# Value products of an attention step: two visits instead of three in a hand-written TensorE order

## The reference

```
x = x + attention(layernorm(x))      # 16 heads of 8 channels, causal, ALiBi
x = x + ffn(layernorm(x))            # gate, 8 experts, all of them summed
attention: scores = q k^T / sqrt(8) + slope_h * key position, causal mask, softmax, times v, w_proj
ffn: logits = z gate_w^T + b, rms-normed, softmax at temperature 0.5, the top gate g;
     y = sum over experts of (gelu(z w1_e + b1_e) w2_e + b2_e) * g / (g + 1e-6)
```

## Time and profile before

| what | value |
|---|---|
| time, median of 3 runs | 320.37 us (320.12 to 320.97) |
| profiled execution, its time | 320.51 us |
| its span, first to last instruction | 318.7 us |
| busy: PE, DVE, ACT, POOL | 296.8, 205.4, 193.7, 85.5 us |
| mean granted TensorE clock | 0.963 of full speed |
| value products L795 on PE | 512 matmul records, 42.3 us busy |
| chain that ended last: PE, DVE | 78%, 11% of the span |

### The profile page before, as it was taken

One profiled execution on the slowest core, in us unless ns is written; L12 is line 12 of the kernel. 1 busy time (PEld: TensorE's weight loads), 2 busy tenths in 40 slices (PEclk: granted clock), 3 DMA queues, 4 the chain that ended last, 5 costly groups with the idle time before them and its releaser, 6 DMA issues.

```text
span 318.7 us, 5649 instructions
## 1 busy us (share of the span) xinstructions
PE 296.8 (93%) x1830; PEld 195.8 (61%) x1831; DVE 205.4 (64%) x817; ACT 193.7 (61%) x323; POOL 85.5 (27%) x213
## 2 busy tenths in 40 slices
PE   7658799999969999999999999999999999999993
PEld 2535456666646666667666676657666765657871
DVE  5538489777877768554877786556776721267871
ACT  6561244646447568758567396857487877535462
POOL 3449321511133055002321172020300500700250
PEclk9795599999999999999999999999999999999998
DMA  6254300130300013002200131002001000000101
GB/s 185 90 148 143 117 2 0 44 114 5 101 18 0 2 38 126 1 0 54 66 5 0 34 97 66 2 17 69 0 4 36 1 4 0 2 0 1 33 2 33
DMA packets 12525, 13.24 MB, mean 42 GB/s; under 512 B 2064, under 2 KB 9104, under 8 KB 12240
## 3 DMA queue, kind: packets, MB, share of 16 engines
q1 hardware_dynamic: 11376, 11.70, 11.9%
q0 software_dynamic: 1024, 1.05, 1.6%
q10 hardware_dynamic: 96, 0.13, 0.2%
HBM read 5.14 MB, written 1.05 MB: 19 GB/s over the span
## 4 chain that ended last, share of the span: by engine, by line
PE 78%; DVE 11%; DMA 3%; issue 2%; POOL 2%; ACT 1%; SPq 1%; DVEq 0%; POOLq 0%; ACTq 0%
PE ffn_bank L863 14%; PE a_ring L770 12%; PE v_ring L748 12%; PE pv_bank L795 11%; PE a_ring L776 5%; PE a_ring L696 5%; DVE unused L1101 5%; PE a_ring L698 4%; PE a_ring L697 4%; DMA q_stack<-q_lo 1%; PE v_ring L824 1%; DMA q_stack<-m_lo 1%; PE v_ring L757 1%; PE v_ring L808 1%; DMA x_in<-x 1%
## 5 line engine op out<-in xcount | busy, mean ns | idle before, releaser
L1101 DVE CUSTOM_DVE_ANT_0 unused<-v_ring,cst 128x512 bf16<-128x512 f32 (+3 forms) x256 | 112.1, 487 | 51.8 <-PE v_ring L748 47.5
L570 ACT ACTIVATE probs<-a_ring 128x512 f32<-128x512 f32 (+1 forms) x192 | 92.3, 526 | 67.1 <-PE a_ring L776 66.0
L748 PE MATMUL v_ring<-k_stack,q_stack 128*128 128x512 f32 (+3 forms) x256 | 88.3, 416 | 5.4 <-DMA q_stack<-q_lo 3.2
L770 PE MATMUL a_ring<-q_stack,k_stack 128*128 128x512 f32 (+3 forms) x256 | 76.2, 357 | 2.0 <-DMA q_stack<-m_lo 2.0
L748 PEld LDWEIGHTS v_ring<-k_stack,q_stack 128*128 128x128 f32 x256 | 48.4, 205 | 25.9 <-issue 15.8
L587 ACT ACTIVATE hidden<-a_ring,cols_sb 128x512 f32<-128x512 f32 x64 | 43.3, 688 | 29.4 <-PE a_ring L698 29.0
L863 PE MATMUL ffn_bank<-hidden,w_sb 128*128 128x512 f32 x100 | 51.9, 604 | 0.9 <-ACT hidden L587 0.9
L770 PEld LDWEIGHTS a_ring<-q_stack,k_stack 128*128 128x128 f32 x256 | 46.0, 194 | 9.5 <-issue 5.6
L776 PE MATMUL a_ring<-score_mask,ident_bf 128*128 128x128 bf16 (+1 forms) x192 | 47.8, 250 | 0.0
L795 PE MATMUL pv_bank<-probs,v_ones 128*32 128x256 f32 (+3 forms) x512 | 42.3, 440 | 0.0
L334 POOL DMA_DIRECT2D k_stack<-k_lo x32 | 18.1, 568 | 56.4 <-PE a_ring L776 51.7
(11 more groups left out here) (123 smaller groups left out, 346.9 us busy)
## 6 DMA issues: line engine op xcount, KB each, us to landing
q_stack<-q_hi SPq DMA_DIRECT2D x8, 256.0 KB
k_stack<-k_hi SPq DMA_DIRECT2D x60, 32.0 KB
x_in<-x SPq DMA_DIRECT2D x4, 256.0 KB, 3.4
hidden<-w SPq DMA_DIRECT2D x1, 1024.0 KB, 7.8
k_stack<-k_lo POOLq DMA_DIRECT2D x32, 32.0 KB, 2.2
q_stack<-q_lo SPq DMA_DIRECT2D x4, 256.0 KB
w_sb<-w SPq DMA_DIRECT2D x1, 1024.0 KB, 5.1
x_res<-x SPq DMA_DIRECT2D x4, 256.0 KB, 2.9
```

What stands on the lines that cost most here:

```text
L570: act.activation(probs[:, n % 2, q, KIND_AT[kind]:KIND_AT[kind] + cols], a_bank()[:, 0:cols], ACT.Exp).then_inc(e_freed, 1)
L748: last = pe.matmul(dst[:, at:at + P * (n + 1)], q_stack[b % 2][:, s, n * P:(n + 1) * P], k_stack[:, s, q, 0:P * (n + 1)], start=True, stop ...
L770: pe.matmul(dst[:, at:at + P * (TB - j)], k_stack[:, s, q, j * P:(j + 1) * P], q_stack[b % 2][:, s, j * P:T], start=(at == 0), stop=False, ...
L1101: ins = dve.tensor_tensor_reduce(unused[:, (uses[0] - 1) % V_BANKS, at:at + cols], bank_[:, at:at + cols], cst[:, C_MASK + T - cols:C_MASK ...
```

## The change

Kinds 1 and 2 of a set's value products are both emitted at place 0 of the next step, one after the other, so that a set has two visits to the value product: kind 0 in its own step, kinds 1 and 2 in the next. Kind 0, which EARLY_PLAN had at place 11, is at place 12 in both plans.

```diff
 EARLY_PLAN = {
     "max": (-1, 0, 2, 3, 4, 5, 6, 8, 8, 9, 11, 11), "take_max": (12,),
-    "exp": (4, 4, 5, 6, 8, 8, 9, 11, 11, 13, 14, 14), "pv": (11, 15), "pv_last": (0,),
+    "exp": (4, 4, 5, 6, 8, 8, 9, 11, 11, 13, 14, 14), "pv": (12,), "pv_last": (0, 0),
 }
 LATER_PLAN = {
     "max": (-1, -1, 2, 3, 4, 5, 6, 7, 8, 9, 10, 11), "take_max": (13,),
-    "exp": (4, 5, 6, 7, 8, 9, 10, 10, 12, 13, 14, 15), "pv": (12, 15), "pv_last": (0,),
+    "exp": (4, 5, 6, 7, 8, 9, 10, 10, 12, 13, 14, 15), "pv": (12,), "pv_last": (0, 0),
 }
...
                         for kind in planned(b, s, k, "pv"):
                             pv(b, s, kind)
-                        if planned(b, s, k, "pv_last") and n >= 1:
-                            pv((n - 1) // SETS, (n - 1) % SETS, KINDS - 1)
-            pv(B - 1, SETS - 1, KINDS - 1)
+                        for i in planned(b, s, k, "pv_last"):
+                            if n >= 1:
+                                pv((n - 1) // SETS, (n - 1) % SETS, 1 + i)
+            pv(B - 1, SETS - 1, 1)
+            pv(B - 1, SETS - 1, 2)
```

## The result

The changed kernel took 321.81 us in the median of 20 runs, the kernel before beside it 320.74 us; the ratio is 1.0036 with an interval of 1.0024 to 1.0048, which is 0.8 to 1.5 us more. The forecast was 322.5 us, +2.0 by its sum. The profiled execution took 322.29 us with a span of 320.5 us, which is 1.8 us longer than the span before; but of these 0.77 lie ahead of all that was changed: the mask matmul of exponential unit 8 in step 0 starts at 42.43 instead of 41.66, and up to there both lists of PE are the same. From that start to the end of the span are 278.07 us, before 318.7 - 41.66 = 277.04: the change itself costs **1.03 us** in the trace; spans are printed to 0.1 us, so this is good to about 0.05.

What follows compares the result with a forecast made beforehand. PE was taken to bound the kernel from 95.8 us, PE and DVE in turn in steps 0 to 4. Terms 0.40 + 1.17 + 0.42 + 0.55 + 0 - 0.52 = +2.02 gave 322.5 us, range 321.0 to 323.7.

Steps and rivals of the forecast that it cites:

- the case of no change: Whole kernel: a difference under 0.3% (0.96 us), not to be told from none; chance 0.13.
- signs of being wrong: Prediction wrong if the transpose of maxima doesn't wait or step 1 loses under 1 us; too low if PE's clock falls.
- the rival in which DVE's backlog holds the start of step 2: DVE's backlog in step 1, not q, leads: the 1.17 goes, +0.85, 321.4 us; within the no-change chance of 0.13.
- step 0: Kind 0 behind the transpose +0.82 on PE, merged boundary -0.26, DVE's hole of 0.09 taken up: about +0.40 us.
- step 1: Kind 0's whole visit falls uncovered behind the transpose, making q's projection late; merged boundary's gain hidden: +1.17 us.
- step 2: PE +0.82 makes y's transpose and DVE's b2 reduction late; unit 0 of the maxima waits for DVE: +0.42 us.
- steps 3 and 4: Step 3: +0.81 - 0.26 = +0.55 us, none taken up; step 4: +1.01 on PE, hidden by its 1.45 us wait for z.
- boundaries into steps 7 and 11: Two merged boundaries in the saturated stretch, where DVE has time: -0.52 us.
- The pushes: Delays on PE in steps 0 to 4 from kind 0 behind the transpose: 0.82, 1.17, 0.82, 0.81, 1.01 us.
- The entry: Time on PE from the float32 transpose of the maxima to the value product behind it: 0.20 us, bounds 0.16 to 0.28.
- Merging: One visit for kinds 1 and 2 at six boundaries between steps spares PE 0.26 us each, bounds 0.22 to 0.30.
- The fall of the clock: New holes in steps 0 to 4 take PE's clock to 1.2 GHz for one 8 us slice: 326.5 us; chance 0.04.

## Why the prediction was right, and where its sizes were off

The direction and the mechanism held, and so did the range, but only as it was widened for the case of no change: the bounds of the sum alone, +1.6 to +2.6 or 322.0 to 323.1 us, miss the 321.81. One of the prediction's own signs of being wrong, less than 1 us lost in step 1, came true by a hair (0.96). And by the number alone the rival in which DVE's backlog holds the start of step 2 (+0.85) lies nearer than the forecast; what rules it out is that step 1 lost its 0.96, and 0.95 when it alone was changed. Two readings of the prediction were off without weight for the sum: the clock row is full from the sixth slice on, not the fifth, and the chain has x16 alone five times, not six (the entry into step 2 is not on it; the timeline has it there at 58.36 us).

Of the terms, by the table (the change against before):

| term | forecast | measured |
|---|---|---|
| step 0 | +0.40 | +0.10 |
| step 1 | +1.17 | +0.96 |
| step 2 | +0.42 | +0.14 |
| steps 3 and 4 | +0.55 | +0.51 - 0.06 |
| boundaries into steps 7 and 11 | -0.52 | -0.60 |
| all | +2.02 | +1.03 |

**The pushes were right.** From unit 8's mask to exponential unit 9, kind 0 and the transpose take 44.41 - 42.43 = 1.98 us in step 0, where they took 42.84 - 41.66 = 1.18: +0.80, forecast 0.82. In step 1 unit 9 starts at 57.07 instead of 55.02; less the 0.87 that step 1 came in late (the transpose of maxima starts at 55.86 instead of 54.99), +1.18, forecast 1.17. The entry was taken at 0.20 and is 0.20 and 0.21.

**What was mis-sized is how much of a push is given back ahead of the next wait**, the part "What of it reaches the end".

- Step 0: unit 2 of the maxima was 0.47 late on PE (47.23 - 45.99 - 0.77), not 0.56. The rest is "a hole of 0.09 us". The next operation of DVE can start with the accumulator's read, not behind it (both at 49.65 here), so the hole between 48.50 and 48.67 is 0.17, and another 0.10 stood ahead of xn (49.29 to 49.39 before, both at 50.26 now). 0.38 - 0.27 = 0.11.
- Step 2: I let the reduction of b2 be late by the whole push and end before unit 0 of the maxima. Of the push of 0.84 at the transpose of y (67.37 before, 70.04 now, less 1.83) only 0.64 was left at DVE's rden (68.21 and 70.68), which started 0.24 us behind m_lo before; 1.83 is the lateness at the step's mask (67.73 against 65.90). And the reduction is at 71.75, unit 0 at 71.82, 0.07 behind its start. So DVE is late by 71.82 - 69.88 - 1.83 = 0.11. PE, which I had bounded by 0.56, gets back 0.40, the wait for a bank: from unit 2 to the exponentials are 73.65 - 72.96 = 0.69 us, before 1.09 (the two lines below). Neither of my bounds held it; the 0.56 left out the bank's wait that I had counted in step 0.

```profile
70.58 1.25 PE L748 MATMUL v_ring<-k_stack,q_stack 128*128 128x256 f32 x4
71.67 0.45 PE L770 MATMUL a_ring<-q_stack,k_stack 128*128 128x512 f32 x1
```

- Step 1: q_full is late by 60.49 - 58.66 = 1.83, which is 0.96 on top of 0.87. Of the 1.18, PE gets back 0.13 between two exponential units that now start 0.22 us apart (58.70 and 58.92), before 0.35 (56.64 and 56.99). ACT had run k_hi just ahead of them before; that this is the cause was only read off the timeline, and the rest of the 0.22 was not followed.
- Merging: forecast 0.26 a boundary, measured 0.30 at the two late ones. In steps 2 and 3 the versions with and without it differ by 0.55 and 0.33 where kind 0 stands ahead.

**Step 4** was right in the trace: kind 0 behind the transpose alone adds nothing there (275.57 against 275.53). **The fall of the clock**, a rival with a chance of 0.04, showed in one trace, with 2.36 us. Runs with a mean clock under 0.960 are 22 of 74 over the kernels that have kind 0 behind in any of steps 0 and 2 to 4 (0 of 6 in the one that doesn't merge), and 1 of 107 over the others (68 of them runs of the kernel before). With the limit at 0.962 and that value counted in, it is 27 of 74 against 15 of 107. The counts suggest that the waits bring such runs about; they do not show it. Where in these runs the clock was low is open, since only one of them was profiled, and taking the wait out of step 4 did not stop them. The six low runs of the change (322.76 to 322.92 us) also lift its median: without them it would be 321.50, 0.76 above before (whose runs beside it have no clock on record). That the medians' +1.07 comes so near to the trace's +1.03 is in part chance.

**The best version** is the change without the move: kind 0 at place 11, kinds 1 and 2 merged, 318.91 us, ratio 0.9942 against the kernel before.

## What to carry to other kernels

Before you move a block of work in an engine's list, ask what wait it covers where it stands: kind 0 took 1.0 us either way, but ahead of the transpose it ran while DVE finished, and behind it the engine stood. When a plan is read as "one visit less in each step", count in the trace how many visits there are: nine of fifteen were together already. And follow a push up to the next wait of every engine, holes included: the pushes of steps 0 to 4, 4.6 us in the forecast, came as forecast in steps 0 and 1, yet 2.5 us of them reached the end.

## What the runs showed of the hardware

- A value product in column tiles starts 0.16 us behind a 128-column mask matmul and 0.20 to 0.21 behind the float32 transpose, where other matmuls follow such a mask after 0.04 in two of three cases (43.05 to 43.09 us in the trace before; 67 of 100). One visit less, which is one change into and out of the tiles, is worth 0.30 us of a saturated PE (16.71 to 16.41).
- DVE's next operation can start at the start of the read of the accumulator (49.65 and 49.65); in the trace before it does so behind 170 of 256 reads.
- The granted clock fell from full to half within step 4 of one execution, at about 90.7 us, and was back at full by 98 us. PE had waited 1.27 us up to 89.03 and was in a wait of 0.77 us when it fell; between 89 and 92 us it was busy 2.20 of 3.00 us. The changed kernel, with waits of 1.26 and 0.77 at the same places, kept the full clock in both of its traces, so these waits by themselves do not settle it. The Trainium skill (TensorE: Matmul & The Clock Gate, HAM oscillation) tells of falls by idle gaps between bursts of matmuls, and the section behind it (A second HAM failure mode) of falls by frequent small idles between groups of matmuls. No run here shows which of the two this fall was.
